# Moving four weight conversions, a table, a store and the first tiles of a two-layer transformer kernel

## The reference, cut to what matters

```python
x = x + L0_xattn(norm(x), ctx)   # causal, 16 heads of 16, softmax over 77 keys, then @ Wp
x = x + L0_ffn(norm(x))          # mixture of experts: 8 experts, top 2 by softmax(x @ router_w.T),
                                 # renormalised; each is gelu(x @ w1[e]) @ w2[e], 256 -> 1024 -> 256
x = x + L1_xattn(norm(x), ctx)   # 16 heads, per-head 16x16 projections, softmax(energy / 16), @ Wo.T + bo
x = x + L1_ffn(norm(x))          # low rank: gelu(x @ U1 @ V1 + b1) @ U2 @ V2 + b2
```

## Time and profile before

| | us |
|---|---|
| median of 3 runs (lowest, highest) | 1058.36 (1057.31, 1061.56) |
| the profiled execution | 1060.01 |
| its span, first to last instruction | 1058.0 |
| PE busy | 910.3 (86%) |
| DVE busy | 621.1 (59%) |
| ACT busy | 512.5 (48%) |
| POOL busy | 423.3 (40%) |

### The profile page before, as it was taken

The page is one execution under the profiler, slowest core; times in us unless marked ns, Lnnn a source line. Parts: engine busy times, 40 slices in busy tenths (PEclk is TensorE's granted clock), DMA queues, the critical chain, the costliest instruction groups (busy, mean ns, idle before and its releaser), DMA issues. The chain is left out here.

```text
span 1058.0 us, 23850 instructions
## 1 busy us (share of the span) xinstructions
PE 910.3 (86%) x7874; PEld 627.0 (59%) x7874; DVE 621.1 (59%) x1484; ACT 512.5 (48%) x865; POOL 423.3 (40%) x592
## 2 busy tenths in 40 slices
PE   5799999997027999999999999995479888879996
PEld 3445656554016889898988989874124444445552
DVE  4567888876795444454444444322768888645561
ACT  1478888875311333323333333342266666645663
POOL 2377777762102423333221222212865665104451
PEclk9789999999557999999999999998568999999999
DMA  6323444334420111112111121112324222000212
GB/s 181 72 77 99 137 125 133 111 102 148 163 79 20 54 49 45 57 41 61 41 49 53 42 61 41 51 46 70 100 70 112 67 71 56 1 1 5 54 45 61
DMA packets 73727, 75.42 MB, mean 71 GB/s; under 512 B 22730, under 2 KB 66874, under 8 KB 73626
## 3 DMA queue, kind: packets, MB, share of 16 engines
q1 hardware_dynamic: 67146, 56.31, 17.9%
q0 software_dynamic: 6480, 17.70, 6.5%
HBM read 51.64 MB, written 22.34 MB: 70 GB/s over the span
## 5 line engine op out<-in xcount | busy, mean ns | idle before, releaser
L1496 DVE CAST hh_e<-h_e 128x512 f16<-128x512 f32 x128 | 59.4, 464 | 178.1 <-ACT h_e L1446 105.3
L1347 PE MATMUL up_ps<-xT_e,experts 128*128 128x256 f16 x512 | 139.6, 273 | 0.7 <-DVE xT_e L1488 0.6
L1361 PE MATMUL y_ps<-experts,hh_e 128*128 x512 | 139.6, 273 | 0.0
L1362 PE MATMUL y_ps<-experts,hh_e 128*128 x512 | 139.6, 273 | 0.0
L1348 PE MATMUL up_ps<-xT_e,experts 128*128 128x256 f16 x512 | 139.6, 273 | 0.0
L1363 PE MATMUL y_ps<-experts,hh_e 128*128 x512 | 139.6, 273 | 0.0
L1349 PE MATMUL up_ps<-xT_e,experts 128*128 128x256 f16 x512 | 139.6, 273 | 0.0
L1273 POOL COPY idx_e<-token 128x2 int32 (+2 forms) x39 | 22.5, 577 | 286.4 <-PE xT_ps_e L1322 237.0
L1446 ACT ACTIVATE h_e<-up_ps 128x512 f32<-128x512 f32 x128 | 76.4, 597 | 87.5 <-PE up_ps L1349 87.5
L1498 DVE TENSOR_TENSOR hh_e<-h_e,hh_e 128x512 f16<-128x512 f32 x128 | 88.6, 692 | 4.4
L1763 ACT ACTIVATE prob_a<-sT_ps_a 77x1024 f32<-77x1024 f32 x64 | 64.9, 1015 | 42.1 <-PE sT_ps_a L1667 42.1
(11 more groups left out here) (328 smaller groups left out, 2115.0 us busy)
## 6 DMA issues: line engine op xcount, KB each, us to landing
experts<-in_L_ffn_w SPq DMA_DIRECT2D x22, 512.0 KB, 4.1
y_scratch<-y_e SPq DMA_DIRECT2D x32, 256.0 KB, 3.4
x<-in_x SPq DMA_DIRECT2D x32, 128.0 KB, 3.3
experts<-in_x SPq DMA_DIRECT2D x64, 64.0 KB, 2.5
x_scratch<-x SPq DMA_DIRECT2D x16, 256.0 KB, 2.5
xh_scratch<-xn SPq DMA_DIRECT2D x16, 256.0 KB, 2.8
w_r<-in_L_ffn_w SPq DMA_DIRECT2D x8, 512.0 KB, 4.3
x_a<-x_scratch SPq DMA_DIRECT2D x32, 128.0 KB, 2.6
```

The costliest lines, as they stand in the source:

```text
L1347: mm(out, w[0], xT[0][:, c, 0:W_], start=c == 0, stop=False)
L1361: mm(out, a[0], w[0], start=m == 0, stop=False)
L1362: mm(out, a[0], w[1], start=False, stop=False)
```

## The change

1. `attend_first`: the zeroing of `qcat` goes from DVE to POOL, ACT no longer waits for DVE's zeroing of `v_ps`, and PE gets dummy matmuls in steps -5 to -2. At the end, the store of tiles 26 and 27 goes ahead of the loads of chunks 22 and 23 on SP, and DVE converts chunk 21 ahead of tile 30's result.
2. `route` and `experts`: the low halves of the last four chunks and the ten operations for the tiles' experts go to the start of `experts`; loads are paired on semaphores.
3. `attend`: only two gathers stand ahead of the first deviation instead of four, the addition of `bo` lags by eight tiles, PE starts with 52 dummy matmuls and has eight more per early tile, score 1 goes ahead of the fourth term, the transposed maxima go to the upper half of bank `pr`, and DVE takes maximum 0 between the reciprocal and the division.

```diff
# attend_first, SP
                 residual(GROUPS - 1, 1)
+                store(NT // 2 - 3)
                 weights(LENT_CHUNKS + 4)
                 weights(LENT_CHUNKS + 5)
-                store(NT // 2 - 3)
# attend_first, POOL, DVE and ACT
+                nc.gpsimd.memset(qcat[:, :, :, :], 0.0).then_inc(qcat_ok, 1)
+                pool.wait_ge(qcat_ok, 1)
                 for k in STEPS:
-                        if k == -4:
-                            pool.wait_ge(v_ok, 1)
-                act.wait_ge(v_ok, 1)
-                nc.vector.memset(qcat[:, :, :, :], 0.0)
# attend_first, PE (in step k)
+                def awake(count):
+                    for i in range(count):
+                        mm(sT_ps[:, 0, 0:D], G["ident16"][:, :], G["khi"][0][:, 0, 0:D], start=True, stop=True)
                     if tile(k + 4):
                         queries(k + 4, k)
+                    if k in (-4, -3):
+                        awake(6)
                     if tile(k + 5):
                         rows_transposed(k + 5, k)
+                    if k in (-5, -4, -3, -2):
+                        awake(6)
# attend_first, DVE, end
+                    if i == 2:
+                        weights(LENT_CHUNKS + 3)
                     result(n)
                     result_statistics(n)
                     normed_result(n - 1)
-                    weights(LENT_CHUNKS + 1 + i)
+                    if i != 2:
+                        weights(LENT_CHUNKS + 1 + i)
# route: SP, ACT, DVE (SOON = 4)
-                    after(sp, wlo_ok, c - WB + 1)
+                    after(sp, wlo_ok, c // 2 * 2 + 2 - WB)
-                    act.wait_ge(w_in[c % WB], 16 * (c // WB + 1))
+                    act.wait_ge(w_in[c // 2 % 2], 32 * (c // WB + 1))
-                    if q + 2 < CHUNKS:
+                    if q + 2 < SOON:
                         weights(q + 2)
...
+                dve.wait_ge(wlo_ok, SOON)
# experts, PE
-                places = [place(0)]
                 awake(24)
+                pe.wait_ge(place_ok, 1)
+                places = [place(0)]
                 transpose(0)
-                awake(8)
+                awake(16)
+                pe.wait_ge(wlo_ok, CHUNKS)
# experts, DVE (experts_of_tiles holds the ten operations that stood in route)
+                experts_of_tiles()
+                for c in range(SOON, CHUNKS):
+                    weights(c)
                 rows(0)
# attend
-        mT_ps = v_ps[:, 0:D].bitcast(F16)
+        mT_ps = pr_bank[:, D:2 * D].bitcast(F16)
# attend, POOL
-                for f in range(3):
+                LAG = 8
+                for f in range(2):
                     gather(f)
                 for f in range(NT):
-                    if f + 3 < NT:
-                        gather(f + 3)
+                    if f and f + 1 < NT:
+                        gather(f + 1)
...
-                    if f > 0:
-                        biased(f - 1)
+                    if f >= LAG:
+                        biased(f - LAG)
# attend, PE: heads_out, maxima_transposed, scores_by_key, projection, the loop
-                    pe.wait_ge(mT_ok, min(k // 4 + 1, GROUPS))
-                    after(pe, oe_ok, 4 * g - 1)
+                    after(pe, mT_ok, g)
+                    after(pe, x3_ok, 4 * g - 5)
                     for term in range(4):
+                        if term == 3:
+                            pe.wait_ge(mT_ok, g + 1)
+                            if tile(k + 5) and k + 5 not in EARLY:
+                                scores(k + 5, 1)
+                    pe.wait_ge(mT_ok, min((n + 5) // 4 + 1, GROUPS))
+                awake(52)
                 for k in STEPS:
                     if f in EARLY:
+                        awake(2)
                         for i in range(4):
                             scores(f, i)
+                        awake(6)
# attend, DVE (sums is the reciprocal, heads the division)
                     if tile(n):
-                        heads(n)
+                        sums(n)
                     if late:
                         maximum(f, 0)
+                    if tile(n):
+                        heads(n)
+                    if late:
                         maximum(f, 1)
```

More of the change, by code:

```diff
@@ L66 @@
 FIRST = CC["early"][0]
+SOON = 4
 FIRST_CHUNKS, LENT_CHUNKS = 24, 18
@@ L528, in attend_first @@
                                       "x1_ok"))
-        ch1, var1_ok, rstd1_ok, xn_ok, lo_ok, ve_ok, ve1_ok, whi_ok, wlo_ok = (
-            L.sem(f"{n}_0") for n in ("ch1", "var1_ok", "rstd1_ok", "xn_ok", "lo_ok", "ve_ok", "ve1_ok", "whi_ok", "wlo_ok"))
+        ch1, var1_ok, rstd1_ok, xn_ok, lo_ok, ve_ok, ve1_ok, whi_ok, wlo_ok, qcat_ok = (
+            L.sem(f"{n}_0") for n in ("ch1", "var1_ok", "rstd1_ok", "xn_ok", "lo_ok", "ve_ok", "ve1_ok", "whi_ok", "wlo_ok", "qcat_ok"))
         ident = G["const"][:, CC["ident"][0]:CC["ident"][1]]
@@ L897, in low @@
                     dve.wait_ge(qhi_ok, f + 1)
+                    if f == 0:
+                        dve.wait_ge(qcat_ok, 1)
                     after(dve, qT_done, f - 3)
@@ L1035, in route @@
         tot, inc, pos, tmp = (L.sb(f"{n}_r", et) for n in ("tot", "inc", "pos", "tmp"))
-        nb, ends, base, single, rest, last, split, jump = (
-            L.sb(f"{n}_r", [P, E]) for n in ("nb", "ends", "base", "single", "rest", "last", "split", "jump"))
+        nb, base, rest, split, jump = (L.sb(f"{n}_r", [P, E]) for n in ("nb", "base", "rest", "split", "jump"))
+        ends, single, last = G["ends"], G["single"], G["last"]
         nbi, pairs_i = L.sb("nbi_r", [P, E], I32), L.sb("pairs_i_r", [P, E], I32)
@@ L1052, in route @@
         WB = 4
-        w = L.sb("w_r", [P, WB, HID])
-        w_in = [L.sem(f"w_in{i}_r") for i in range(WB)]
-        whi_ok, wlo_ok = L.sem("whi_ok_r"), L.sem("wlo_ok_r")
+        w, whi_ok, wlo_ok = G["w_late"], G["whi_late"], G["wlo_late"]
+        w_in = [L.sem(f"w_in{i}_r") for i in range(2)]
         CHUNKS = 4 * E - FIRST_CHUNKS
@@ L1253, in experts @@
         QF = FULL * QS
+        ends, last, single, cmp_, cnt, found = (G[n] for n in ("ends", "last", "single", "cmp", "cnt", "found"))
+        found_ok, place_ok, wlo_ok = L.sem("found_ok_e"), L.sem("place_ok_e"), G["wlo_late"]
+        CHUNKS = 4 * E - FIRST_CHUNKS
         def tiles(eng, step):
@@ L1604, in _ @@
                         .then_inc(shift_ok, 1)
-                    if f > 0:
-                        biased(f - 1)
-                biased(NT - 1)
+                    if f >= LAG:
+                        biased(f - LAG)
+                for f in range(NT - LAG, NT):
+                    biased(f)
                 for n in range(4):
@@ L1706, in rows_transposed, with awake @@
                     last.then_inc(t_done, 1)
+                def awake(count):
+                    for i in range(count):
+                        mm(pr_ps, G["ident16"][:, :], G["khi"][1][:, 0, 0:D], start=True, stop=True)
+                awake(52)
                 for k in STEPS:
@@ L1719, in _ @@
                         scores_by_key(k)
-                    if late:
-                        scores(f, 1)
                     if tile(n):
@@ L1906, in _ @@
                 unit_normed(nc, dve, G, 3)
-                heads(NT - 4)
-                heads(NT - 3)
+                for n in REST[0:2]:
+                    sums(n)
+                    heads(n)
                 for n in REST:
                     if n + 2 < NT:
+                        sums(n + 2)
                         heads(n + 2)
@@ L1958, in feed_forward_loads, with allocate_tables @@
     sp.dma_start(b2[:, :], A["L1_ffn_b2"][None, :].broadcast_to([P, D])).then_inc(G["ff_in"], 16)
+def allocate_tables(nc, ctx, G):
+    L = Place(nc, ctx)
+    G["w_late"], G["whi_late"], G["wlo_late"] = L.sb("w_late", [P, 4, HID]), L.sem("whi_late"), L.sem("wlo_late")
+    for n in ("ends", "single", "last"):
+        G[n] = L.sb(n, [P, E])
+    G["cmp"], G["cnt"], G["found"] = L.sb("cmp", [1, ET, E]), L.sb("cnt", [1, ET]), L.sb("found", [1, ET])
 def allocate_last(nc, ctx, G):
@@ L2184, in program @@
                 attend_first(nc, A, G)
-            route(nc, A, G)
-            experts(nc, A, G)
+            with ExitStack() as inner:
+                allocate_tables(nc, inner, G)
+                route(nc, A, G)
+                experts(nc, A, G)
         with ExitStack() as inner:
```

45 lines of the change are left out of this document (28 added, 17 removed).

## The result

| | before | after |
|---|---|---|
| median, us (lowest to highest) | 1058.7 (1057.31 to 1061.56), 4 runs | 1043.3 (1036.95 to 1049.18), 4 runs |
| the profiled execution | 1060.01 | 1037.76 |
| its span | 1058.0 | 1035.7 |

The changed kernel takes 0.985 of the time before (95% interval 0.981 to 0.989). Its four runs lie at two levels: 1037.0 and 1037.8, 1048.9 and 1049.2. The profiled one is of the lower level, so the forecast's steps are read first in that one (1060.0 to 1037.8, forecast 1036.2), and the upper level is a question of its own.

The account below looks back on a forecast made before the run. Blocks run in turn: DVE bounds route, PE experts, neither alone attend. Gains 1.2 + 4.4 + 6.0 + 4.2 + 2 + 6 = 23.8 us took the median 1058.4 to 1034.6, stated as 1035; range 1026 to 1046.

Parts of the forecast that it names:

- A: Start of layer 0's attention: waits for DVE's zeroings go, second f16 copy at 44.0; gain 1.2 us, bounds -1.5 to 3.
- B: End of layer 0's attention: earlier store ends DVE's wait for tile 30; gain 4.4 us, bounds 3.2 to 4.6.
- C: Route into experts: earlier token table, first real matmul waits for DVE, not dummies; gain 6.0 us, bounds 4.3 to 6.5.
- D: First tiles of layer 1's attention: tile 0's norm 3.1 us earlier, next five 1.1; gain 4.2, bounds 3 to 5.
- E: Steps 0 to 4 of layer 1's attention: score 1 passes one term, half-clock time similar; gain 2 us, bounds -2 to 5.
- F: Full steps of layer 1's attention: new order and the maxima's new bank; gain 6 us, bounds 1 to 12.
- 0.65 x 6 = 3.9: Full steps: moving the transposed maxima to another bank saves 0.65 us in each of six steps.
- if it stays up: Start of layer 0's attention: if dummies keep PE's clock full, the second f16 copy comes at 44.0 instead of 45.16.
- Bound A (-1.5): Start of layer 0's attention: loss of 1.5 us if the clock falls anyway and 36 dummies stand in PE's way.
- rival (c): Order costs what it saves, half-clock stretch grows, layer 0's start loses 1: gain 15.6 us, time 1043; chance 0.19.
- (a): DVE bounds the full steps, which gain 14.2 us instead of 6: time 1027; chance 0.12.
- (d): Slower: gathers one tile ahead land late and delay each of 24 steps; 1066 us at a 6.0 landing; chance 0.03.

Follow-up runs that it names:

- seams_only: The kernel before with parts 1 and 2 of the change alone, layer 1's attention as before: median 1053.9 us, ratio 0.995.
- hold_both: The changed kernel with 39 more dummy matmuls in layer 0's attention and 35 in steps 0 to 4 of layer 1's attention: 1032.5 us, ratio 0.973.
- early_hold: The changed kernel with 39 more dummy matmuls in gaps of layer 0's attention, steps -4, -2 and -1: 1036.7 us, ratio 0.978.
- mT_back: The changed kernel with the transposed maxima back in the bank of the outputs, with their two waits as before: 1043.5 us, ratio 0.985.
- hold_clock: The changed kernel with 35 more dummy matmuls in steps 0 to 4 of layer 1's attention: median 1038.8 us, ratio 0.981.
- attend_only: The kernel before with part 3 of the change alone, the changed attend: median 1049.5 us, ratio 0.990.
- after_again: The changed kernel run again without an edit: six runs from 1035.8 to 1048.4 us, ratio 0.984; the profiled one took 1047.0.
- held_store_back: hold_both with the store of tiles 26 and 27 behind the two loads and chunk 21's conversion behind tile 30's result: 1035.1 us, ratio 0.978.

## Why the prediction was right or wrong

| term | forecast | profiled executions | undone or alone, on the chip |
|---|---|---|---|
| A start of layer 0's attention | 1.2 | 2.95 (1037.8) or -5.0 (1047.0) | without the dummies 4.0 (trace) |
| B its end | 4.4 | 4.42 | 2.7 (trace 3.26) |
| C route to experts | 6.0 | 5.98 | 4.8 (trace 4.7) |
| D first tiles of attend | 4.2 | 3.99 | 4.2 |
| E steps 0 to 4 | 2 | -1.4 | |
| F full steps | 6 | 6.4 | order 3.7 in all, 0.46 per four steps; bank 0.15 per four steps |
| sum | 23.8 | 22.3 | |

The profiled column adds up by the leads of the events named above: 7.37 at the last store, 13.39 at attend's first load, 17.38 at tile 5's norm, 15.95 at tile 10's, 22.3 at the end. That 22.3 comes so near 23.8 is in part luck: A gave 1.75 more than forecast and E 3.4 less.

**Right.** B, C and D, to 0.2 us each in the traces, B and C with the steps as forecast. In D, tile 0's norm gained 2.55 and not 3.1, and the next five tiles 1.44 and not 1.1. B and C were read against a dear execution. The store took 6.5 us to land in the one of before, but with the same order put back the wait was 3.15 and not 4.47 (the lower bound, 3.2, is the better value). And 1.1 of C's 6.0 is when the clock came back among the dummies, an accident of the profiled execution.

**F: the total right, its split wrong.** The prediction gave 0.65 in a group of four steps to the bank and about 0.3 to the order. Alone, undoing the bank costs 0.15 and undoing the order 0.46; both as before cost 22.46 - 21.48 = 0.98. So 0.37 shows only when both are undone: each hides the other. The step that failed is "0.65 x 6 = 3.9" for the bank. The wait is there (0.78) and leaves its own step as forecast (6.11 to 5.57 us), but the prediction had next to nothing for what the move costs: the step behind it goes from 5.17 to 5.57, as ACT's copy for the projection, which was to cause a wait of "up to 0.1", comes 0.39 later there. About 0.7 of the 6.4 lies behind the last tile's norm, where the kernel before had a stretch at half clock (933.2 to 936.6) and the changed one had none.

**E: the sign was wrong.** "About as long a half-clock time as before" was right: between the norms of tiles 5 and 12 it was 31 us, before 30. Its place was not: before, 8.2 of them (763.6 to 771.8) lay under tiles that POOL paced at 4.1 us each, now 1.9. And "score 1 passes a term, 0.43 at half clock, five steps" fails, since at half clock PE is itself the bound (27.02 of 30 us busy) and an order on PE wins nothing: such a step took 6.7 where a full-clock one had taken 5.16 before. seams_only shows it: with the order as before and the clock at half, the three tiles from the norm of tile 7 to that of tile 10 took 20.3 us, in the changed kernel 20.6. With the clock held those seven tiles took 33.6 us (hold_both) against 40.4 (after) and 39.4 (before): the stretch was worth 6.9 us.

**A: right up to the second copy, wrong on the clock.** The waits that went give 1.2, as forecast. The rest of the 2.95 is what the prediction had as its upper bound, the half clock of 66 to 73 gone, less about 1.0 for the new stretch at 55.9. But "if it stays up" made a full clock the condition of the gain. Without the dummies the clock was at half from 41 to 55 and the block as fast, as POOL sets the pace there. What the prediction had no term for is that with the dummies the clock fell at 55.5, when the steps become full, and came back after 4 us or after 10 to 28. That is the upper level, 8.0 of 9.3 us, and the likely reason why the median of the changed kernel's ten runs is near 1044 while the lower five lie at 1036 to 1041. Bound A (-1.5) didn't hold it. The median of 1043.3 is 8 us above the stated 1035 and equals rival (c)'s figure, 1043, but only partly by its way. (c) had -2 for steps 0 to 4, which came true (-1.4), but also a loss of 1 here, where the two executions gained 3 or lost 5, and 4 for the full steps, which gained 6.4. (a) fell, as DVE still idles for 0.20 a step, and (d) too: a plain step takes 5.17 where late gathers would have made it 6.5.

That these dummies make the levels is well shown from one side: with 39 more, the 30 runs of six kernels (early_hold, hold_both and the four with a part undone) show one level each, with spreads of 1.1 to 5.4 us. From the other side, none at all, it rests on five runs (4.9 us apart). In mT_back and hold_clock, whose layer 0 is the changed one, the runs fill the range between the levels, as the stretch of 10 us in mT_back's profile would have it. That attend_only's runs spread too (1042 to 1055), without such dummies, is not explained by it. Not tried by themselves: the 52 dummies ahead of attend's first tile and the eight per early tile, and in layer 0 the move of the zeroing apart from ACT's wait.

## What to carry to other kernels

Dummy matmuls are worth what the stretch behind them is bound by: in the filling steps of this pipeline, where another engine sets the pace, a half clock was free, and dummies that ended before the steps were full went with a fall of the clock where it costs. Fill the gaps up to and into the first full steps (the best kernel here), or else leave the dummies out; and look at the granted clock of several executions, since one profile can show the cheap case only. An edit's gain read from one trace holds that execution's accidents; undoing it in the quietest version gives its price, within the runs' spread. And a wait that is removed can come back one step later: read the step behind it too.

## What the runs showed of the hardware

- A half clock can last while PE is busy all the time. In after_again PE was busy for 22.50 of 22.50 us at half clock (59.5 to 82), by a trace that models the ends of matmuls, while in the first profile the same program had it back after 4 us. The Trainium skill ("TensorE: Matmul & The Clock Gate", "What's actually happening") says that activity releases the throttle; the 27.3 us here (55.4 to 82.7) disagree with it, the 4 us of the other execution agree.
- What PE did ahead of the fall at 55.5: busy for 7.15 of 9.5 us, its longest idle piece 1.26 us (46 to 55.5). With gaps filled (early_hold), 8.27 of 9.5, it didn't fall. The same page ("A second HAM failure mode: psum-queue depth-cycling") says that frequent short idle times between groups of matmuls can make the clock oscillate between its two levels, and these two traces agree so far: it fell with the short gaps and not with them filled. That kernel's gaps come from its cycling through PSUM banks, which no run here tried.
- Zeroing 4096 f16 elements per partition took POOL 3.52 us; the same bytes took DVE 1.76 as 2048 uint32. That is 0.86 ns per element on both.
- A stretch of 3.5 to 4 us at half clock turns up in most executions at places that differ (241 to 257, 905 to 937), and it costs time. In the five executions of the changed block's end with one at 241 to 257 the last store is issued 50.1 us behind the last f16 copy, in the five others of it and in seams_only 48.5 to 48.7 (held_store_back, whose end differs, left out). From tile 31's norm to the end of the span it is 146.9 to 147.4 us in the seven executions without one, 147.9 to 149.0 in the six with one at 905 to 937, and 150.3 in the one with two.
